# Tile 0's LoRA product in split fp32r, its gather index written in place, and the small matrices loaded and adjusted earlier

## The reference, cut to what matters

```python
# x: (64, 32, 512) fp32, cond: (64,) in 0..15, adapter: (64,) in 0..23
W0 = weights0[cond]                                # (64, 32, 32)
x  = x + einsum('bct,bcd->bdt', x, W0)             # mix the 32 channels
A, Bm = lora_As[adapter], lora_Bs[adapter]         # (64, 512, 16), (64, 16, 512)
x  = x + einsum('bti,oi->bto', x, W) + b \
       + 2 * einsum('btr,bro->bto', einsum('bti,bir->btr', x, A), Bm)
```

## Time and profile before

| what | us |
|---|---|
| median of 3 runs | 84.73 |
| lowest, highest | 84.17, 86.11 |
| the profiled execution's own time | 84.99 |
| its span in the trace | 83.2 |
| TensorE busy in the span | 79.4 (95%) |
| VectorE busy | 60.2 (72%) |
| ScalarE busy | 52.3 (63%) |
| GpSimd busy | 33.7 (41%) |

### The profile page before, as it was taken

One profiled execution on the slowest core, in us unless ns is written; L12 is line 12 of the kernel. 1 busy time (PEld: TensorE's weight loads), 2 busy tenths in 40 slices (PEclk: granted clock), 3 DMA queues, 4 the chain that ended last, 5 costly groups with the idle time before them and its releaser, 6 DMA issues.

```text
span 83.2 us, 2011 instructions
## 1 busy us (share of the span) xinstructions
PE 79.4 (95%) x524; PEld 72.2 (87%) x524; DVE 60.2 (72%) x158; ACT 52.3 (63%) x179; POOL 33.7 (41%) x75
## 2 busy tenths in 40 slices
PE   4999999999999999999999999999999999999970
PEld 2378897899899999999999999999999999999850
DVE  2059765977789687777878787978777777869560
ACT  1553947954867675957666766667585867665620
POOL 6118842871171717080625344351708071304300
PEclk9999999999999999999999999999999999999999
DMA  1899786796987888765768766576764526030334
GB/s 15 287 357 311 203 233 200 211 278 195 335 254 182 262 199 227 194 212 201 176 195 213 219 195 234 156 264 183 230 188 150 174 85 189 17 119 0 126 126 126
DMA packets 16141, 16.07 MB, mean 193 GB/s; under 512 B 10241, under 2 KB 10626, under 8 KB 16130
## 3 DMA queue, kind: packets, MB, share of 16 engines
q1 hardware_dynamic: 14016, 11.67, 47.3%
q0 software_dynamic: 1248, 4.06, 15.7%
q10 hardware_dynamic: 866, 0.21, 1.1%
HBM read 11.74 MB, written 4.19 MB: 191 GB/s over the span
## 4 chain that ended last, share of the span: by engine, by line
PE 82%; SPq 6%; DMA 4%; DVE 2%; issue 2%; ACT 0%; DVEq 0%
PE z_ps L570 49%; PE z_ps L607 9%; PE z_ps L650 5%; PE ht_ps L561 5%; DMA a_raw<-in_lora_a 4%; PE y_ps L622 4%; PE y_ps L618 4%; PE y_ps L620 4%; SPq L237 3%; PE ht_ps L594 2%; PE ht_ps L659 1%; DVE y_sb L555 1%; SPq L227 1%; SPq L234 1%; SPq L257 1%
## 5 line engine op out<-in xcount | busy, mean ns | idle before, releaser
L570 PE MATMUL z_ps<-wa,x_hi 128*128 128x288 f32 (+2 forms) x240 | 50.2, 301 | 0.0
L570 PEld LDWEIGHTS z_ps<-wa,x_hi 128*128 128x128 f32 x240 | 37.9, 188 | 2.0 <-issue 0.5
L570 PE MATMUL z_ps<-wa,x_lo 128*128 128x288 f32 (+2 forms) x120 | 35.2, 295 | 0.0
L570 PEld LDWEIGHTS z_ps<-wa,x_lo 128*128 128x128 f32 x120 | 22.5, 188 | 0.0
L309 POOL CAST m_hi<-m_raw 128x128 fp32r<-128x128 f32 x16 | 4.9, 303 | 35.4 <-ACT m_raw L346 35.4
L300 POOL DMA_INDIRECT b_raw<-in_lora_b,b_index_slot x16 | 16.8, 1048 | 4.4 <-POOL b_index_slot L298 4.4
L490 DVE TENSOR_TENSOR z_lo<-z_ps,z_hi 128x256 fp32r<-128x256 f32 x31 | 11.8, 420 | 6.3 <-ACT z_hi L390 6.3
L390 ACT CAST z_hi<-z_ps 128x256 fp32r<-128x256 f32 x31 | 10.2, 376 | 9.5 <-PE z_ps L607 9.5
L346 ACT COPY m_raw<-w_raw 32x32 f32 x64 | 13.8, 216 | 2.1 <-DVE w_raw L522 1.1
L449 DVE TENSOR_TENSOR x_lo<-x_raw,x_hi 128x512 fp32r<-128x512 f32 x14 | 9.7, 691 | 3.5 <-ACT x_hi L358 3.5
L470 DVE TENSOR_TENSOR b_lo<-b_raw,b_hi 128x512 fp32r<-128x512 f32 x15 | 10.4, 692 | 0.6
(11 more groups left out here) (57 smaller groups left out, 78.3 us busy)
## 6 DMA issues: line engine op xcount, KB each, us to landing
out<-y_sb SPq DMA_DIRECT2D x15, 256.0 KB, 2.5
x_raw<-in_xt SPq DMA_DIRECT2D x14, 256.0 KB, 3.0
a_raw<-in_lora_a SPq DMA_DIRECT2D x60, 32.0 KB, 2.6
first_sb<-in_first SPq DMA_DIRECT2D x2, 384.0 KB, 3.7
first_sb<-in_first SPq DMA_DIRECT2D x3, 256.0 KB, 5.2
b_raw<-in_lora_b,b_index_slot POOLq DMA_INDIRECT x16, 3.7
bias_sb<-in_bias SPq DMA_DIRECT2D x1, 256.0 KB, 3.0
a_raw<-in_lora_a ACTq DMA_DIRECT2D x4, 32.0 KB
```

The lines of the kernel that those rows point to most:

```text
L570: done = nc.tensor.matmul(target, (x_hi, x_lo)[part[0]][u % 2][:, k, :], moving(part[1]), start=k == 0 and part == HH, stop=k == KC - 1 an ...
```

## The change

Tile 0's LoRA product becomes the same split fp32r product as in the other tiles. The masked h of tile 0 is rounded on ACT into the upper 64 partitions of `ht_sb[0]` (`round_ht0`), and the rest goes to the lower 64 (`rest_ht0`, DVE); the gather of tile 0 brings the 64 rows of B twice (128 partitions), these are split into `b_hi` and `b_lo` (`round_b(0)`, `rest_b(0)`), and four matmuls (b_hi, b_lo, for two halves) take the place of two fp32 ones. `first_h` is moved in front of the three `LH` matmuls of tile 1's chunks 0 to 2. SP issues the load of W0 right behind the five first pieces, ahead of the wait for the ids; DVE adds its identity ahead of the lo parts of x1, where it stood behind `mask_ht(0)`. DVE writes the index column of tile 0's gather straight into its buffer (one instruction for it, one for the 15 others), so POOL copies none for tile 0. The waits of later gathers are counted anew, with the same meaning but for tile 3, whose gather now waits for b_lo of tile 0.

```diff
@@ sync
             for n in range(len(PIECES) - 1):
                 load_first(n)
+            sp.dma_start(w0_raw[:, :, :], w0).then_inc(w0_loaded, 16)
             sp.wait_ge(ids_loaded, 16)
             load_a(1)
             load_x(2)
-            sp.dma_start(w0_raw[:, :, :], w0).then_inc(w0_loaded, 16)
             load_a(2)
@@ gpsimd, gather_b(u)
-            pool.wait_ge(b_index_ready, 1)
...
-                if u == NB:
-                    pool.wait_ge(lora_done, 2)
-                elif u > NB:
-                    pool.wait_ge(b_ready, u - NB)
-                rows = slice(0, JR if u == 0 else P)
-                pool.tensor_copy(b_index_slot[s][:, :], b_index[:, u:u + 1]).then_inc(b_index_copied, 1)
-                pool.wait_ge(b_index_copied, u + 1)
+                    pool.wait_ge(b_ready, u - NB + 1)
+
+                pool.wait_ge(b_index_ready, 1 if u == 0 else 2)
+                if u > 0:
+                    pool.tensor_copy(b_index_slot[s][:, :], b_index[:, u:u + 1]).then_inc(b_index_copied, 1)
+                    pool.wait_ge(b_index_copied, u)
@@ scalar
+            def round_ht0():
+                act.wait_ge(ht0_masked, 1)
+                act.copy(ht_sb[0][0:JR, :], ht0_sb[:, :]).then_inc(ht0_hi_ready, 1)
...
             round_x(2)
+            round_b(0)
+            round_ht0()
             round_a(2)
@@ vector
+            def rest_ht0():
+
+                dve.wait_ge(ht0_hi_ready, 1)
+                nc.vector.tensor_tensor(ht_sb[0][JR:P, :], ht0_sb[:, :], ht_sb[0][0:JR, :],
+                                        ALU.subtract).then_inc(ht_ready, 1)
...
-                nc.vector.tensor_scalar(b_index[:, :], ids_p_sb[:, 0:TILES], float(R), r_of_p[:, 0:1],
+                nc.vector.tensor_scalar(b_index_slot[0][:, :], ids_p_sb[:, 0:1], float(R), r_of_p[:, 0:1],
+                                        ALU.mult, ALU.add).then_inc(b_index_ready, 1)
+                nc.vector.tensor_scalar(b_index[:, 1:], ids_p_sb[:, 1:TILES], float(R), r_of_p[:, 0:1],
                                         ALU.mult, ALU.add).then_inc(b_index_ready, 1)
@@ tensor, lora(u, half)
-                if u == 0:
-                    pe.wait_ge(b_gathered[0], 16)
-                    nc.tensor.matmul(z_of(0, half), ht0_sb[:, :], b_raw[0][0:JR, cols(half)], start=False,
-                                     stop=True, skip_group_check=True).then_inc(lora_done, 1)
-                    return
-                pe.wait_ge(b_ready, u)
+                pe.wait_ge(b_ready, u + 1)
```

More of the change, by code:

```diff
@@ L145, in lora_residual_program @@
         ht_computed = sem("ht_computed")
+        ht0_masked = sem("ht0_masked")
+        ht0_hi_ready = sem("ht0_hi_ready")
         ht_ready = sem("ht_ready")
@@ L514, in _ @@
                 rest_w(k)
+            dve.wait_ge(w0_loaded, 16)
+            nc.vector.tensor_tensor(w0_raw[:, :, :], w0_raw[:, :, :],
+                                    ident[0:C, 0:C].rearrange("p (a d) -> p a d", a=1).broadcast_to([C, S0, C]),
+                                    ALU.add).then_inc(w0_plus_i, 1)
             rest_x1(0)
@@ L668, in _ @@
                 half_chunk(1, k, 0, (HH, HL))
-            pe.wait_ge(x_ready, 1)
-            for k in range(2):
-                half_chunk(1, k, 0, (LH,))
             pe.wait_ge(x_hi_ready, 2)
@@ L674, in _ @@
             half_chunk(1, 2, 0, (HH, HL))
+            first_h()
             pe.wait_ge(x_ready, 2)
-            half_chunk(1, 2, 0, (LH,))
-            first_h()
+            for k in range(3):
+                half_chunk(1, k, 0, (LH,))
             pe.wait_ge(w_hi_ready, KC)
```

16 lines of the change are left out of this document (7 added, 9 removed).

## The result

The changed kernel takes 85.18 us (median of 20 runs, 84.54 to 85.66), the kernel before 84.60 in the same sessions: ratio 1.0068, interval 1.0043 to 1.0092. The forecast was 0.43 us faster; it is 0.58 slower. Each execution has its own time and its span. Over all 20 of them the changed kernel's span has a median of 83.1 us (82.5 to 83.6), and 2.06 us (2.02 to 2.15) lie outside it. The profiled execution: own time 85.45, span 83.3.

What follows compares the result with a forecast made beforehand. PE, busy 95%, was taken to bound the kernel, held up once by SP's load chain to A(4). The earlier first_h gave -0.43 us, the other parts nothing at the end: median 84.73 to 84.3, range 83.6 to 85.1.

Steps and rivals of the forecast that it cites:

- `first_h` earlier: PE, warm-up: first_h starts 0.43 us earlier, at 9.65; SP's load_a(3) and tile 2's LoRA follow by 0.43.
- LoRA of tile 0: PE: four split matmuls take 0.48 us where two fp32 ones took 1.06, shortening PE's own path by 0.58.
- W0 and the operands: DVE, ACT and gather before tile 0's LoRA: early W0 costs nothing; PE waits 0 to 0.3 us for operands.
- Behind it: ACT after the new LoRA's operands: A(2) rounded until 12.5, then m and z of tile 0; costs 0 to 0.2 us.
- More bytes: DMA: the earlier, doubled gather and W0 delay what follows by their bytes, 0.24 and 0.47 us, already counted.
- the 1.79 us outside: Time outside the profiled span, added unchanged to the forecast span of 82.8 us to give 84.6.
- B: Rival: the wait at tile 2's LoRA vanishes and PE's own path decides, -0.91 us, 83.8; chance 0.13.
- A: Rival: full DMA engines set when A(4) lands, so the load chain doesn't move; 84.7 us, chance 0.17.
- C: Rival: tile 0's gather comes late, PE waits 1.4 us in tile 1, a loss of 0.5; 85.2 us, chance 0.08.
- D: Rival: W0 lands late, at 9.9, holding DVE and the LoRA operands; no gain, 84.8 us, chance 0.07.

Runs made afterwards that it cites:

- f3: The kernel before with one change, first_h moved ahead of the three LH matmuls of tile 1's chunks 0 to 2; 84.49 us, ratio 0.9973.
- h2: The changed kernel with A(1) used in place of A(2) to A(4), whose loads are still issued but not waited for; 84.57 us, ratio 1.0000.
- h1: The changed kernel with A(1) used in place of A(2), whose load is still issued but not waited for; 84.71 us, ratio 1.0020.
- h3: The kernel before with A(1) used in place of A(2) to A(4), whose loads are still issued but not waited for; 84.80 us, ratio 1.0014.
- e3: The changed kernel with the load of W0 and its identity addition back in their old places; 85.96 us, ratio 1.0146.
- e1: The changed kernel with build_m(0) ahead of round_a(2) on ACT; 84.93 us, ratio 1.0031.
- f1: e1 with tile 2's gather of B issued behind the split of m(0) on POOL; 85.91 us, ratio 1.0140.
- f2: e1 with four buffers for A instead of three, so load_a(3) waits for nobody; 84.74 us, ratio 1.0000.
- f4: e1 with the identity added to W0 on DVE behind the lo parts of A(1), the load staying early; 84.96 us, ratio 1.0038.
- e4: The changed kernel with 64 gathered rows for tile 0 and without the product with the lo part of its masked h; 84.73 us, ratio 1.0013.
- g1: The changed kernel with tile 0's old fp32 LoRA and 64 gathered rows; W0, first_h and the index stay changed; 84.77 us, ratio 0.9986.
- g3: The changed kernel with tile 0's index column copied by POOL as before; 85.25 us, ratio 1.0040.
- e2: The kernel before with one change, tile 0's gather brings all 128 rows (64 twice); 84.74 us, ratio 1.0006.
- g4: The changed kernel with first_h and the LH matmuls in their old order; 85.77 us, ratio 1.0111.
- i1: The changed kernel without the loads of A for tiles 2 to 15, all using tile 1's A; 85.70 us, ratio 1.0108.
- h4: The kernel before with first_h ahead of the three LH matmuls and four buffers for A; 84.39 us, ratio 0.9973.

## Why the prediction was wrong

- *`first_h` earlier*: right. It starts at 9.67 (said: 9.65), and SP issues `load_a(3)` 0.42 earlier (11.39 against 11.81; said: 0.43). Alone it brings 0.25 us in the span (`f3`, ratio 0.9973, not clear of no change), not 0.43: all that PE had to win there were the 0.33 it stood waiting. And in `f3` `load_a(3)` is issued no earlier than before (11.82), though `first_h` starts 0.21 earlier.
- *LoRA of tile 0*: right in size, wrong in what becomes of it. The forecast was 0.48 us in place of 1.06, a gain of 0.58. It takes 0.48 in `h2`, where PE comes to it without a listed wait. In after it takes 0.58, a gain of 0.48: PE stands just in front of it (0.44 us from the start before, where `h2` has 0.14), and the first of the four matmuls takes 0.23 us instead of 0.12.
- *W0 and the operands*: right. DVE adds at 8.83, the x1 parts are in time, the gather is no trouble, PE starts the LoRA at 12.80 instead of 12.66 (said: a wait of 0 to 0.3; the starts show about 0.3).
- ***Behind it* is the step that failed.** It said "A(2) is rounded until 12.5", from ACT's own sum, and let A(2) have no landing of its own. The sum was right, ACT is free for A(2) at 11.90. *More bytes* had priced the extra traffic on A(1) and x of tile 2 and stopped there. A(2) was rounded only from 12.81, because it landed at 12.79, 1.4 us later than the old ACT had it, from the same issue (7.28). Behind it m and z are late (14.36 instead of 13.86), and PE waits 0.92, where 0 to 0.2 had been put down. With that wait taken out (`h1`) z is rounded at 13.18, tile 2 starts 0.33 us behind the last matmul of tile 1 where 0.15 is usual, and the time falls by 0.4 us: the rest of this step was right. The row that could have warned me was not among those shown: the old ACT took A(2) at 11.35 after a wait of 0.55. The 1.09 us of wait behind it gave A(2) its only room there. I read that wait as W0's alone, and the change takes W0 out of it, so a later A(2) reaches z at once.
- **A second term was carried over unmeasured**: "the 1.79 us outside" the span. It is 2.06 in after, and 1.96 to 2.09 in all twelve kernels with the split LoRA; it is 1.73 to 1.77 in the seven experiments with the fp32 LoRA and in the kernel before. Of the 0.58 us by which the change is slower, half is this. No row of the old trace could show it.
- The sum in the profile's terms: forecast -0.43 in the span and 0 outside; measured +0.25 (83.1 against 84.60 - 1.75 = 82.85, with the 1.75 of the later sessions) and +0.31. Between the two traces, up to the matmul behind tile 2's LoRA (22.75 against 22.59, +0.16): the LoRA of tile 0 starts 0.14 later and is 0.48 shorter; from its end to that of tile 1's LoRA it is 0.84 longer (4.89 against 4.05), mostly the wait for z; the next round is 0.34 shorter (4.48 against 4.82), which is the wait for A(4). With A(2) to A(4) unwaited the span is 0.4 below before. That is near the forecast's 0.43, in part by luck: `h3` shows that the wait for A(4), on which the 0.43 rested, did not give its 0.33 back.
- The rivals: none. What B named came about, the wait for A(4) vanished, but because PE now comes later there, having stood for A(2). A, C and D did not occur. 85.18 is beyond the range by 0.08; the 0.4 of A(2) or the 0.31 outside the span would each, alone, have left it inside.

What stays open is why A(2) lands late. It does in after (12.79) and in `e3` (by 13.10). In `e1`, `f1`, `f2` and `f4` ACT comes to it too late (12.73 to 13.41) to tell. It was on time with fewer gathered bytes (`e4`, `g1`), with a later gather (`g3`) and with the doubled gather in the old kernel (`e2`), which speaks for a gather of tile 0 that is both earlier and larger. But `g4` has both, issued at 6.27, and takes A(2) by 12.01 without waiting, though in an execution far above its median:

```profile
12.01 0.49 ACT L372 CAST wa<-a_raw 128x128 fp32r<-128x128 f32 x2
```

A rival is tile 1's gather, 256 KB. In after and `e3` it is issued early and quickly, from 8.63 to 9.60 and from 8.05 to 9.38. In `e4`, `g1` and `g4` the same instruction starts at 8.63 to 8.69 too but lasts until 11.11 to 11.36, and in before, `e2` and `g3` it starts at 8.78 to 8.94. No run changes that gather alone, so neither cause is shown. Landings also differ between kernels with the same issue: A(3), issued at 11.19 in both, is taken at 15.55 in `e2` and at 16.73 in `e4`, each after a wait for it. That is one trace each, so I do not lean on any single one.

What makes the 0.31 us outside the span isn't known either. It isn't the number of instructions (2016 in after, 1821 in `i1`, 2.06 and 2.08 us), nor the two semaphores that after declares more (`g1` declares them too, with 1.77). It goes with the two added instructions of ACT or with what they wait on, which no run separates; `g3`, with 1.96, is 0.1 below the others.

The best versions are `f3` and `h4`, 0.9973 with intervals that just include 1: `first_h` early, and nothing else of the change (`h4` with a fourth buffer for A).
